# A state-space block scanned in halves: output products after each scan, the next batch's delta directly behind the second scan

## The reference

```python
A = -jnp.exp(A_log)
x_dbl = u @ x_proj_w.T
dt, Bm, Cm = jnp.split(x_dbl, [DT_RANK, DT_RANK + D_STATE], axis=-1)
delta = jax.nn.softplus(dt @ dt_proj_w.T + dt_proj_b)
dA = jnp.exp(delta[..., None] * A)
dBu = delta[..., None] * Bm[:, :, None, :] * u[..., None]
# for each step: h = dA_t * h + dBu_t ;  y = sum over n of h[d, n] * C_t[n]
```

## Time and profile before

| | us |
|---|---|
| median of 3 runs (3629.53 to 3649.26) | 3643.72 |
| the profiled execution | 3659.85 |
| its span, first to last instruction | 3658.1 |
| first scan of the block starts | 65.7 |
| last scan starts | 722.1 |

### The profile page before, as it was taken

The page is one execution under the profiler, slowest core; times in us unless marked ns, Lnnn a source line. Parts: engine busy times, 40 slices in busy tenths (PEclk is TensorE's granted clock), DMA queues, the critical chain, the costliest instruction groups (busy, mean ns, idle before and its releaser), DMA issues. The chain is left out here.

```text
span 3658.1 us, 52097 instructions
## 1 busy us (share of the span) xinstructions
PE 2766.2 (76%) x15862; PEld 1904.2 (52%) x15863; DVE 2182.0 (60%) x4412; ACT 1507.2 (41%) x4235; POOL 875.8 (24%) x1280
## 2 busy tenths in 40 slices
PE   3777777641969999989335886999997699986085
PEld 2444444331956666656214754666665466654074
DVE  5999999930336666657675033787873387734044
ACT  4566566510216666545221122666662244422011
POOL 4333333425530000022103000111100122201643
PEclk7888888755979999989655587999998799986598
DMA  9100000003740000000004000000000000000166
GB/s 359 71 0 0 0 0 0 0 12 96 222 117 1 0 0 0 1 6 0 6 0 55 0 0 13 1 0 0 0 1 6 13 1 0 0 6 0 47 180 177
DMA packets 106792, 127.72 MB, mean 35 GB/s; under 512 B 30050, under 2 KB 79284, under 8 KB 102580
## 3 DMA queue, kind: packets, MB, share of 16 engines
q1 hardware_dynamic: 97460, 107.27, 9.9%
q0 software_dynamic: 9216, 19.02, 1.5%
HBM read 68.84 MB, written 57.41 MB: 35 GB/s over the span
## 5 line engine op out<-in xcount | busy, mean ns | idle before, releaser
L650 DVE TENSOR_TENSOR_SCAN s_state<-s_decay,s_state 128x4096 f32<-128x4096 f32 x32 | 276.3, 8675 | 0.0
L555 PE MATMUL s_ysumP<-s_state,ident 128*128 128x512 f32 x512 | 262.2, 656 | 0.0
L1110 ACT ACTIVATE s5a_prob<-s5a_scoreP,s5a_nmax 128x256 f32<-128x256 f32 x512 | 235.1, 475 | 41.8 <-DVE s5a_nmax L1284 41.6
L1110 ACT ACTIVATE s2s_prob<-s2s_scoreP,s2s_nmax 128x128 f32<-128x128 f32 (+1 forms) x512 | 208.3, 427 | 45.5 <-DVE s2s_nmax L1282 45.1
L462 ACT ACTIVATE s_decay<-s_delta,s_aneg 128x255 f32<-128x255 f32 x512 | 208.4, 493 | 17.7 <-DVE s_delta L626 17.6
L1284 DVE TENSOR_REDUCE s5a_nmax<-s5a_scoreP 128x4 f32<-128x1024 f32 x128 | 156.7, 1224 | 67.3 <-PE s5a_scoreP L1209 66.9
L2632 POOL DMA_INDIRECT parts<-m_y,m_to x160 | 153.1, 957 | 174.4 <-DVE m_y L2723 142.5
L1282 DVE TENSOR_REDUCE s2s_nmax<-s2s_scoreP 128x2 f32<-128x256 f32 (+1 forms) x256 | 130.8, 553 | 106.4 <-PE s2s_scoreP L1204 105.9
L2801 PE MATMUL m_turnP<-ident,m_xin 128*128 128x128 f32 x160 | 33.2, 291 | 212.6 <-DMA m_w<-in_m_w 209.5
L660 DVE TENSOR_TENSOR s_state<-s_state,s_bcP 128x1024 f32<-128x1024 f32 x128 | 147.7, 1216 | 38.3 <-PE s_bcP L502 36.7
L502 PE MATMUL s_bcP<-s_bc,s_sel 96*128 96x256 bf16 x512 | 83.9, 297 | 112.3 <-DVE s_state L660 99.3
(11 more groups left out here) (584 smaller groups left out, 6922.2 us busy)
## 6 DMA issues: line engine op xcount, KB each, us to landing
sorted<-blank SPq DMA_DIRECT2D x32, 1105.0 KB, 28.0
m_w<-in_m_w SPq DMA_DIRECT2D x120, 256.0 KB
m_xin<-sorted SPq DMA_DIRECT2D x80, 130.0 KB
m_row<-parts SPq DMA_DIRECT2D x32, 256.0 KB, 5.3
m_w<-in_m_w SPq DMA_DIRECT2D x40, 128.0 KB
s_mats<-s_scratch SPq DMA_DIRECT2D x4, 1024.0 KB, 16.2
parts<-m_y,m_to POOLq DMA_INDIRECT x160
sorted<-m_row,m_idx POOLq DMA_INDIRECT x128, 2.3
```

The lines of the kernel that those rows point to most:

```text
L555: ins = nc.tensor.matmul(ysumP[:], ident[:], state[:, :, n, :], start=(n == 0), stop=(n == NS - 1))
L650: nc.vector.tensor_tensor_scan(cells, flat(decay[c]), cells, 0.0, ALU.mult, ALU.add).then_inc(S["scanned"], 1)
L1110: ins = nc.scalar.activation(prob[i][:, h, a:b], scoreP[i][:, h, a:b], ACT.Exp, bias=nmax[:, p % 4, h, r:r + 1], accum_out=den[s][:, r, 2 ...
```

## The change

- VectorE multiplies a half's states by C directly behind that half's scan: scan 0, four output products, scan 1, then `front4(t + 1)`, then the other four. C is therefore spread once for each half, 12 spreads a batch instead of 8 (`SP`).
- `sums` works on one half and one group, 4 matmuls of 128x256, and stands at other places among the spreads.
- TensorE's front is cut in two: `front_in(t + 1)` (transposes, convolution, residual) behind spread 3, and `front_out(t + 1)` behind `out(t - 1)`.
- ScalarE does `front` and `soft` of the next batch between the 8th and the 9th decay of the second half instead of behind the 16th. It takes over (1 + e) - 1 as two Copy activations (`part`), and its logarithm comes behind all decays. `store` of a batch moves behind the next but one batch's first 16 decays.
- GpSimd's `lost_part` is two instructions instead of three and a hold.

```diff
+    SP = 3 * NG
...
             def lost_part(t):

-                pool.wait_ge(S["em_ready"], t + 1)
-                pool.wait_ge(S["mag_ready"], 4 * t + 4)
-                st.hold(spare)
-                st.do(nc.gpsimd.tensor_scalar(lost[:], em[:], 1.0, -1.0, ALU.add, ALU.add))
-                st.do(nc.gpsimd.tensor_tensor(lost[:], em[:], lost[:], ALU.subtract))
+                pool.wait_ge(S["kept_part"], 2 * t + 2)
+                st.do(nc.gpsimd.tensor_tensor(lost[:], em[:], part[:], ALU.subtract))
                 nc.gpsimd.tensor_tensor(pos[:], pos[:], lost[:], ALU.add).then_inc(S["pos_ready"], 1)
...
+                nc.scalar.activation(part[:], em[:], ACT.Copy, bias=1.0).then_inc(S["kept_part"], 1)
+                ac.wait_ge(S["kept_part"], 2 * t + 1)
+                nc.scalar.activation(part[:], part[:], ACT.Copy, bias=-1.0).then_inc(S["kept_part"], 1)
...
+            def logarithm(t):
+                wait(ac, S["delta_ready"], t)
                 nc.scalar.activation(lg[:], em[:], ACT.Ln, bias=1.0).then_inc(S["lg_ready"], 1)
...
             for t, s, more in batches(ac):
-                first = isinstance(t, int) and t == 0
                 decays(t, 0, 0, NS)
+                if not isinstance(t, int) or t >= 2:
+                    store(t - 2)
                 if more:
                     norm_in(t + 1)
                     unit(t + 1, 1 - s)
-                decays(t, 1, 0, NS // 4)
-                if more:
+                    decays(t, 1, 0, 2)
                     turn_in(t + 1)
-                decays(t, 1, NS // 4, NS)
-                if more:
-                    front(t + 1, 1 - s, None if first else t - 1)
+                    decays(t, 1, 2, NS // 2)
+                    front(t + 1, 1 - s, None if isinstance(t, int) and t == 0 else t - 1)
                     soft(t + 1)
+                    decays(t, 1, NS // 2, NS)
+                    logarithm(t + 1)
                 else:
+                    decays(t, 1, 0, NS)
                     size_out(t - 1)
-                if not first:
-                    store(t - 1)
+            store(NB - 2)
...
+                line = GN * k if k < 2 * NG else GN * (k - NG)
                 for n in range(GN):
-                    ins = nc.tensor.matmul(bcP[k % 2][:, n, :], sel[:, GN * k + n, :], bc3[s][:], start=True, stop=True)
...
-            def sums(t, lo, hi):
-
-                pe.wait_ge(S["bc_used"], t * 2 * NG + NG + hi // GN + (hi % GN > 0))
-                if lo == 0:
+            def sums(t, c, g):
+
+                pe.wait_ge(S["bc_used"], t * SP + (1 + c) * NG + g + 1)
+                if g == 0 and c == 0:
                     wait(pe, S["yT_ready"], t)
-                for n in range(lo, hi):
-                    ins = nc.tensor.matmul(ysumP[:], ident[:], state[:, :, n, :], start=(n == 0), stop=(n == NS - 1))
-                    if n % GN == GN - 1:
-                        ins.then_inc(S["summed"], 1)
+                for n in range(GN * g, GN * g + GN):
+                    ins = nc.tensor.matmul(ysumP[:, c, :], ident[:], state[:, c, n, :], start=(n == 0), stop=(n == NS - 1))
+                ins.then_inc(S["summed"], 1)
...
             for t, s, more in batches(pe):
                 first = isinstance(t, int) and t == 0
                 if not first:
-                    sums(t - 1, 10, 12)
                     carry(t - 1, 1 - s)
                 spread(t, s, 2)
-                if not first:
-                    sums(t - 1, 12, 16)
                 spread(t, s, 3)
+                if more:
+                    front_in(t + 1, 1 - s)
+                spread(t, s, 4)
+                spread(t, s, 5)
                 if not first:
                     out(t - 1)
                 if more:
-                    front(t + 1, 1 - s)
-                spread(t, s, 4)
-                spread(t, s, 5)
+                    front_out(t + 1, 1 - s)
                 spread(t, s, 6)
-                sums(t, 0, 4)
                 spread(t, s, 7)
-                sums(t, 4, 6)
+                sums(t, 0, 0)
+                spread(t, s, 8)
+                sums(t, 0, 1)
+                spread(t, s, 9)
+                sums(t, 0, 2)
+                sums(t, 0, 3)
+                spread(t, s, 10)
+                spread(t, s, 11)
+                sums(t, 1, 0)
                 if more:
                     spread(t + 1, 1 - s, 0)
-                sums(t, 6, 8)
+                sums(t, 1, 1)
                 if more:
                     spread(t + 1, 1 - s, 1)
-                sums(t, 8, 10)
-            sums(NB - 1, 10, 12)
-            sums(NB - 1, 12, 16)
...
-                wait(ve, S["summed"], (t - 1) * NG + g + 1)
+                wait(ve, S["summed"], (t - 1) * 2 * NG + NG + g + 1)
...
-            def outputs(t, g):
-
-                ve.wait_ge(S["bc_ready"], t * 2 * NG + NG + g + 1)
+            def outputs(t, c, g):
+
+                k = (1 + c) * NG + g
+                ve.wait_ge(S["bc_ready"], t * SP + k + 1)
                 if g == 0:
-                    ve.wait_ge(S["scanned"], 2 * t + 2)
-                for c in range(2):
-                    part = state[:, c, GN * g:GN * g + GN, :]
-                    ins = nc.vector.tensor_tensor(part, part, bcP[g % 2][:], ALU.mult)
-                    if c == 0:
-                        st.done(ins)
-                ins.then_inc(S["bc_used"], 1)
+                    ve.wait_ge(S["scanned"], 2 * t + c + 1)
+                part = state[:, c, GN * g:GN * g + GN, :]
+                nc.vector.tensor_tensor(part, part, bcP[k % 2][:], ALU.mult).then_inc(S["bc_used"], 1)
...
                 scan(t, 0)
+                for g in range(NG):
+                    outputs(t, 0, g)
                 scan(t, 1)
-                outputs(t, 0)
-                outputs(t, 1)
-                outputs(t, 2)
-                outputs(t, 3)
                 if more:
                     front4(t + 1, 1 - s)
+                for g in range(NG):
+                    outputs(t, 1, g)
```

More of the change, by code:

```diff
@@ L248, in mamba @@
         lost = sc.sb("lost", [P, 2, L])
+        part = sc.sb("part", [P, 2, L])
         lg = sc.sb("lg", [P, 2, L])
@@ L341, in split @@
                 pool.wait_ge(S["high_ready"], t + 1)
-                wait(pool, S["bc_ready"], (t - 1) * 2 * NG)
+                wait(pool, S["bc_ready"], (t - 1) * SP)
                 st.done(nc.gpsimd.tensor_tensor(bcr[:], bc[:], bc3[s][0:32, :], ALU.subtract))
@@ L433, in front @@
                 wait(ac, S["bc3_ready"], t)
-                wait(ac, S["bc_ready"], (t - 1) * 2 * NG)
+                wait(ac, S["bc_ready"], (t - 1) * SP)
                 nc.scalar.activation(bc3[s][0:32, :], dblP[0:32, 0, :], ACT.Copy).then_inc(S["high_ready"], 1)
@@ L470, in _ @@
             soft(0)
+            logarithm(0)
             for t, s, more in batches(ac):
-                first = isinstance(t, int) and t == 0
                 decays(t, 0, 0, NS)
+                if not isinstance(t, int) or t >= 2:
+                    store(t - 2)
                 if more:
@@ L495, in spread @@
             def spread(t, s, k):
-                r = t * 2 * NG + k
+                r = t * SP + k
                 wait(pe, S["bc_used"], r - 1)
@@ L500, in spread, with front_in @@
                     pe.wait_ge(S["bc3_ready"], t + 1)
+                line = GN * k if k < 2 * NG else GN * (k - NG)
                 for n in range(GN):
-                    ins = nc.tensor.matmul(bcP[k % 2][:, n, :], sel[:, GN * k + n, :], bc3[s][:], start=True, stop=True)
+                    ins = nc.tensor.matmul(bcP[k % 2][:, n, :], sel[:, line + n, :], bc3[s][:], start=True, stop=True)
                 ins.then_inc(S["bc_ready"], 1)
-            def front(t, s):
+            def front_in(t, s):
                 pe.wait_ge(S["xn_ready"], t + 1)
@@ L522, in front, with front_out @@
                 ins.then_inc(S["projected"], 1)
+            def front_out(t, s):
                 pe.wait_ge(S["u_ready"], t + 1)
@@ L547, in carry @@
                 ins.then_inc(S["kept"], 1)
-            def sums(t, lo, hi):
-                pe.wait_ge(S["bc_used"], t * 2 * NG + NG + hi // GN + (hi % GN > 0))
-                if lo == 0:
+            def sums(t, c, g):
+                pe.wait_ge(S["bc_used"], t * SP + (1 + c) * NG + g + 1)
+                if g == 0 and c == 0:
                     wait(pe, S["yT_ready"], t)
-                for n in range(lo, hi):
-                    ins = nc.tensor.matmul(ysumP[:], ident[:], state[:, :, n, :], start=(n == 0), stop=(n == NS - 1))
-                    if n % GN == GN - 1:
-                        ins.then_inc(S["summed"], 1)
+                for n in range(GN * g, GN * g + GN):
+                    ins = nc.tensor.matmul(ysumP[:, c, :], ident[:], state[:, c, n, :], start=(n == 0), stop=(n == NS - 1))
+                ins.then_inc(S["summed"], 1)
             pe.wait_ge(S["setup"], 3)
             pe.wait_ge(S["selected"], 3)
-            front(0, 0)
```

(19 more changed lines are left out.)

6 lines of the change are left out of this document (3 added, 3 removed).

## The result

| | before | after |
|---|---|---|
| median of 20 runs of each, on the same chip (us) | 3636.87 (3623.65 to 3649.26) | 3649.99 (3634.6 to 3661.94) |
| ratio, 95% interval | | 1.0035 [1.0022, 1.0049] |
| the profiled execution | 3659.85 | 3650.2 |
| first DMA issue behind the block (`m_wr`) | 757.22 | 772.24 |

The change costs 0.35%, about 12.7 us; the forecast was +12.5 us, "within 0.5%". As wholes the two profiled executions stand the other way round: in the later stages, where the program is the same, they took 2900.9 us before and 2876.3 after, which the change cannot explain. So the block is compared by its own times: it ends 15.0 us later.

A forecast was written before the change was run, and what follows sets the result against it. VectorE, 92% busy, sets the pace, with about 3 us of waits a batch. 14 x 0.93 - 0.9 + 4.0 - 3.6 = +12.5 us, on the median 3643.72, gives 3656 us (+0.34%); range 3630 to 3682.

The forecast's parts named there:

- wait for spread 0: Before the next batch's first input product, VectorE waits 2.0 us for TensorE's spread behind a slow half-group sum.
- wait before input group 2: Ahead of the gate, VectorE waits 0.9 us for spread 2, behind TensorE's three more half-group sums and carry.
- wait before the second scan: Scan 1 waits 0.95 us for the last eight decays, which now stand behind the next batch's front.
- first scan of batch 0: Before the first delta, GpSimd drops 1.94 + 0.27 and ScalarE adds 1.3: -0.9 us, once.
- first batch: Batch 0's scan 1 waits for decays behind the front's SiLU, a new wait of 4.0 us, once.
- last batch, first scan to gate: With no next front and half the sums done under scan 1, 33.6 us instead of 37.2: -3.6.
- I take slow until 7.0: TensorE's restart behind the second scan runs slow until 7.0 us after that scan's end, delaying the sum before spread 0.
- The decay chain: ScalarE and TensorE work from the gate's table load through SiLU, projections and Copy passes to the last decays: 14.6 us.
- Half-width passes bound by weight loads: Rival, chance 0.16: TensorE's 256-column identity passes take 0.26 instead of 0.215 us, adding 1.5 us a batch; 3677.
- GpSimd caught: Rival, chance 0.14: GpSimd's last addition for `pos` ends 1.1 us behind the second scan and delta waits; 3671.
- TensorE at 2.4 GHz throughout: Rival, chance 0.15: the clock stays up, waits before the gate shrink from 2.9 to about 1.3, period 42.5 or 42.7; 3636.
- VectorE bound by its own work: Rival, chance 0.09: both waits gone and a chain 1 us shorter leave VectorE's own 39.9 + 0.3 us a batch; 3600.

The follow-up runs named there:

- the fourth experiment: The changed kernel with the rounding loss computed on GpSimd in three instructions and a hold, without ScalarE's two Copy passes: 3701.41 us, ratio 1.0108.

## Why the prediction was right

**The place of the waits: right.** The prediction named three and no others: for spread 0, for spread 2 and, before the second scan, for the decays. These are the three in the trace, and the wait before the output products is gone.

**Their sizes: right in the sum, off singly.**

| term (us) | predicted | measured |
|---|---|---|
| wait for spread 0 | 2.0 | 2.8 |
| wait before input group 2 | 0.9 | 0.68 |
| wait before the second scan | 0.95 | 0.68 |
| period | 44.1 | 44.33 |
| 14 steady batches | +13.0 | +15.9 |
| first scan of batch 0 | -0.9 | -2.35 |
| first batch (48.12 against 43.18) | +4.0 | +4.9 |
| last batch, first scan to gate (33.74 against 37.2) | -3.6 | -3.5 |
| sum, in the profiled executions | +12.5 | +15.0 |

The first wait is the mis-sized term. "I take slow until 7.0" (with the scan's end at zero) was 363.9 - 356.0 = 7.9: the restart runs at half clock for 5.4 us, so that all eight passes of the sum are slow and not the first part of them. That is 0.8 us more at spread 0, and it is the 2.8 that the prediction gave for 1.2 GHz throughout; of it 0.2 comes back at the next wait. The decay chain was 0.3 shorter than added up (14.3 to the last decay). Of the Copy passes, for which the trace of before had no row, the value taken, 0.63 each like the exp, is what they take. In the first batch ScalarE's SiLU stood as follows:

```profile
67.88 0.84 ACT L424 ACTIVATE s_u<-s_xmP,s_convb 128x256 f32<-128x256 f32 x2 [2.90 <-PE s_xmP L523]
```

And VectorE's second scan:

```profile
81.67 8.69 DVE L665 TENSOR_TENSOR_SCAN s_state<-s_decay,s_state 128x4096 f32<-128x4096 f32 x1 [4.80 <-ACT s_decay L467]
```

The SiLU comes at 67.9 instead of 70.73; 1.2 of this is that the first convolution took 4.91 us where it took 6.14 before, which isn't the change's doing. Such a difference of about a microsecond stands in the -2.35 too.

**The timed +12.7 against +12.5 is luck within some 2 us.** The sum from the profiles came out 2.5 above the forecast; the timed difference, with an interval of about 5 us either way, fell between them. The forecast's 3656 us stood on a median of 3643.72; in the comparison the kernel before had 3636.87, and the kernel after 3650.

**The rivals.** Half-width passes bound by weight loads: false, (1.89 - 0.38) / 7 = 0.216 us apart at full clock. GpSimd caught: not in this kernel, but by a margin of 1.4 us at the addition's issue; the fourth experiment shows the price when it happens: delta waits 2.5 us, and the batch is 1.75 longer. The Trainium skill, "SBUF — State Buffer", section "Who interferes with whom", has the first to start win; the trace agrees in both directions, 9.33 us for a GpSimd subtraction behind a scan's start and 9.17 instead of 8.69 for a scan behind an addition's. It does not where the GpSimd instruction is tiny: the one of 128x2 at 347.16 ran over the scan's start, and the scan took its 8.69. TensorE at 2.4 GHz throughout: false for the change, since the granted clock over twelve batches only went from 0.83 to 0.85; brought about by idle passes at the restart ahead of the gate alone (granted clock 0.91 over the twelve batches), it gave a period of 42.30, where the rival had 42.5 to 42.7. VectorE bound by its own work: no kernel came to it; it needs about 40 us a batch (39.8 busy in one of 41.07), and no steady batch took less than 41.06. The Trainium skill, "ScalarE: Activation LUTs", section "What ACT_TABLE_LOAD costs", would add about 1.4 us a load; the trace disagrees, the SiLU starts 1.29 us after its load starts.

**What the prediction missed** is the remedy: it treated TensorE's slow restart as given, in both kernels. Taken away at one restart, it is worth 2.0 us a batch in the changed kernel, and 2.1 in most batches of the one before (1.7 over all).

Open: whether fewer idle passes would do, and what number or place of them would keep the clock in every batch. In the kernel before with 48 of them, and with 36 and spread 2 early, the clock fell in some batches all the same.

## What to carry to other kernels

When a wait is for a small piece of TensorE's work right behind a gap, read the granted clock of that stretch before reordering anything: here a reorder of three engines' work cost 0.35%, and idle passes in the gap gave 0.7% in the old order and 0.9% in the new. Work that is moved off one wait lands on the engine that is next to last; walk one batch on each engine's clock to see which, as here ScalarE's decays and TensorE's spreads. A gain that is measured beside one bottleneck may be zero there and three microseconds beside the next (the early delta), so undo parts again after the largest cost is gone.

## What the runs showed of the hardware

- TensorE, idle for 4.5 us, was granted the 1.2 GHz level for 5.4 us on its return. With bf16 passes of 96x256 in the gap it stayed at 2.4 GHz in most batches, but not in all: in the kernel before with 48 passes the clock fell in two of the twelve batches, in one of them while the passes ran.
- A running GpSimd addition of 128x512 holds back a scan on VectorE that is issued under it: 9.17 instead of 8.69 us. The other way round a GpSimd instruction of 0.18 us took 8.05. A GpSimd instruction of 128x2 that ran over the first 0.5 us of a scan (347.16 to 347.87) did not lengthen it (8.69).
- A Copy activation of 128x512 takes 0.63 us on ScalarE, like an exp of that shape.
